# A two-layer transformer kernel: the first expert's weights and rows loaded within attention, and new orders of loads, of GpSimd's steps and of one score sum

## The reference

```
xn = layernorm(x)
x  = x + L0_attn(xn) + L0_ffn(xn)      # low-rank q/kv, rope, causal softmax, 16 heads of 16; 8 experts, top 2, capacity 1280
xn = layernorm(x)
x  = x + L1_attn(xn) + L1_ffn(xn)      # 32 learned patterns, sparsemax over them; 8 experts + shared MLP, masked by top 2

def sparsemax(z):
    z_sorted = -sort(-z); cum = cumsum(z_sorted); k = 1..S
    k_sup = sum(1 + k * z_sorted > cum)
    tau = (cum[k_sup - 1] - 1) / k_sup
    return max(z - tau, 0)
```

## Time and profile before

| | us |
|---|---|
| median of 3 runs | 2135.6 (2132.08 to 2140.5) |
| the profiled execution's own time | 2135.76 |
| its span | 2134.0 |

### The profile page before, as it was taken

The page is one execution under the profiler, slowest core; times in us unless marked ns, Lnnn a source line. Parts: engine busy times, 40 slices in busy tenths (PEclk is TensorE's granted clock), DMA queues, the critical chain, the costliest instruction groups (busy, mean ns, idle before and its releaser), DMA issues. The chain is left out here.

```text
span 2134.0 us, 35062 instructions
## 1 busy us (share of the span) xinstructions
PE 1970.1 (92%) x11874; PEld 1197.7 (56%) x11874; DVE 1537.6 (72%) x3465; ACT 1035.9 (49%) x2246; POOL 517.0 (24%) x932
## 2 busy tenths in 40 slices
PE   7867999999999999999789999996879999999998
PEld 3333333333333333333289999995656777777776
DVE  6858998888888888888045333325669898889983
ACT  3425667777777777777644444443331122221112
POOL 4644223322222222222223333336500000000000
PEclk9968999999999999999989999998889999999998
DMA  5554301111111111110033322215510000000005
GB/s 194 188 155 153 117 16 56 56 42 41 44 43 43 44 43 43 44 43 12 15 110 101 108 85 88 90 45 168 154 45 21 1 20 20 21 20 20 10 11 162
DMA packets 111780, 143.69 MB, mean 67 GB/s; under 512 B 12152, under 2 KB 96768, under 8 KB 111232
## 3 DMA queue, kind: packets, MB, share of 16 engines
q1 hardware_dynamic: 87248, 98.09, 14.2%
q0 software_dynamic: 10400, 31.47, 4.3%
q10 hardware_dynamic: 13968, 12.06, 1.7%
HBM read 85.10 MB, written 56.10 MB: 66 GB/s over the span
## 5 line engine op out<-in xcount | busy, mean ns | idle before, releaser
L830 ACT ACTIVATE at_wt<-at_B 128x512 f32<-128x512 f32 (+3 forms) x1280 | 606.5, 538 | 239.4 <-PE at_B L929 233.4
L1234 DVE TENSOR_REDUCE at_piece_max<-at_A 128x1 f32<-128x512 f32 x768 | 487.3, 683 | 59.4 <-PE at_A L910 57.5
L947 PE MATMUL at_O<-at_wt,at_v 128*32 128x512 f32 (+3 forms) x2560 | 312.3, 540 | 0.0
L735 POOL TENSOR_SCALAR_AFFINE_SELECT at_wt<-at_wt 128x128 f32<-128x128 f32 x512 | 148.0, 294 | 612.9 <-ACT at_wt L830 604.2
L1231 DVE CUSTOM_DVE_ANT_0 at_junk<-at_A,s_hide 128x128 bf16<-128x128 f32 (+3 forms) x512 | 230.2, 487 | 77.4 <-PE at_A L910 77.0
L910 PE MATMUL at_A<-at_k,at_q 96*128 96x512 bf16 (+3 forms) x800 | 275.0, 353 | 8.9 <-DVE at_piece_max L1231 2.6
L929 PE MATMUL at_B<-at_q,at_k 99*128 99x512 bf16 (+3 forms) x800 | 272.7, 348 | 2.0 <-ACT at_wt L830 2.0
L1454 PE MATMUL ex_H<-ex_xT,ex_w_in 128*128 128x256 f32 x1920 | 248.2, 286 | 3.3 <-DVE ex_xT L1561 3.3
L1454 PEld LDWEIGHTS ex_H<-ex_xT,ex_w_in 128*128 128x128 f32 x1920 | 237.4, 193 | 3.6 <-DVE ex_w_out L1566 3.6
L1575 DVE TENSOR_TENSOR ex_h<-ex_act_a,ex_H 128x256 f32<-128x256 f32 x160 | 66.8, 418 | 213.0 <-ACT ex_act_a L1503 212.9
L910 PEld LDWEIGHTS at_A<-at_k,at_q 96*128 96x128 bf16 x800 | 77.6, 97 | 214.4 <-DVE at_piece_max L1234 108.9
(11 more groups left out here) (264 smaller groups left out, 2597.6 us busy)
## 6 DMA issues: line engine op xcount, KB each, us to landing
buf<-at_room POOLq DMA_DIRECT2D x10, 1024.0 KB, 8.9
ex_x<-buf SPq DMA_DIRECT2D x40, 256.0 KB, 2.6
expert_out<-ex_y ACTq DMA_DIRECT2D x40, 256.0 KB, 2.2
ex_raw_in<-in_W_in SPq DMA_DIRECT2D x8, 1024.0 KB, 5.0
q_parts<-parts SPq DMA_DIRECT2D x16, 384.0 KB, 3.4
...
```

The source lines that it names most:

```text
L735: pool.affine_select(block_, block_, [[1, P]], ALU.is_ge, 0.0, base=0, channel_multiplier=-1).then_inc(hidden, 1)
L830: act.activation(wt[(HP * p + h) % NE_][:, q0:CH], pB_of(p, h, u)[:, q0:CH], ACT.Exp, scale=D ** -0.5).then_inc(wt_ready, 1)
L947: pe.matmul(pO[j % 2][rows, q0:CH], vs[n % 3][:, kt // TPC, kt % TPC, :], wt[(HP * p + h) % NE_][:, q0:CH], start=kt < 2 and not late, sto ...
L1234: ins = dve.tensor_reduce(top, pA[slot % NA][:, 0:w], AX.X, ALU.max)
```

## The change

1. Three tiles `raw_in`, `raw_out` and `first_rows` are made ahead of `latents` and live until `experts` ends. In `latents` they are `xn`, two of three `by_cos` and of `by_sin`; in `attention` `q[1]`, `k[1]` and `k[2]`; in `experts` the raw weights and the rows. SP issues expert 0's weight loads and the first two row loads at the end of attention's SP list, once the head pairs that used the tiles are done and all rows are put.
2. First maxima: `pats` gets its own semaphore, so that `pats_turn` waits for it alone; the other nine small loads are waited for from `wq_turn` on. On SP, `mlp_load(3)` to `mlp_load(9)` go ahead of `load(1)`, which is dealt out in four parts between them; `iota` and `below` come after the first max store.
3. GpSimd splits the biases between `low(2)` and `low(6)` and copies the rows before `low(7)`. `low(0)` comes before `diag_q`; the values' product comes after `low(4)`.
4. `layer1`: in the MLP whose DVE list holds the scan, `keep_scores` goes ahead of it.
5. `finish`: Wo shares the semaphore of the first part load.

```diff
-        q = [s["q0"]] + [sb(f"q{i}", [QKS, HP, S], BF16) for i in range(1, 3)]
-        k = [s["k0"]] + [sb(f"k{i}", [QKS, S], BF16) for i in range(1, 3)]
+        q1 = s["raw_in"][:].rearrange("p k n -> p (k n)").bitcast(BF16).rearrange("p (h n) -> p h n", h=HP)
+        k1 = s["raw_out"][:].rearrange("p f e -> p (f e)").bitcast(BF16)
+        k2 = s["first_rows"][:].rearrange("p i t e -> p (i t e)").bitcast(BF16)
+        q = [s["q0"], q1[0:QKS], sb("q2", [QKS, HP, S], BF16)]
+        k = [s["k0"], k1[0:QKS], k2[0:QKS]]
...
             for e in range(NW):
                 mlp_load(e)
-            load(1)
+            for e in range(NW, MLPS):
+                mlp_load(e)
+                if e - NW <= len(RUNS):
+                    load(1, e - NW)
+            max_store(0, 0, M0_SLOT + 2)
             sp.dma_start(iota, d["c_iota"]).then_inc(routing_in, 16)
             sp.dma_start(below, d["c_below"]).then_inc(routing_in, 16)
-            for e in range(NW, MLPS):
-                mlp_load(e)
-            max_store(0, 0, M0_SLOT + 2)
...
+            sp.wait_ge(wt_used, PER_B * (HPAIRS - 2))
+            sp.dma_start(s["raw_in"][:], d["W_in"][0].rearrange("(k p) f -> p k f", p=P)).then_inc(s["w_loaded"], 16)
+            sp.dma_start(s["raw_out"][:], d["W_out"][0].rearrange("(k p) e -> p k e", p=P)).then_inc(s["w_loaded"], 16)
+            sp.wait_ge(wt_used, PER_B * (HPAIRS - 1))
+            for i in range(2):
+                sp.wait_ge(put[i], 16 * 2 * TOPK * (HPAIRS // 2))
+            rows = d["buf"].rearrange("(m t p) e -> m p t e", t=2, p=P)
+            for i in range(2):
+                sp.dma_start(s["first_rows"][:, i], rows[i]).then_inc(s["x_loaded"][i], 16)
...
             def pats_turn():
-                pe.wait_ge(small_in, 16 * 10)
+                pe.wait_ge(pats_in, 16)
...
             def wq_turn():
+                pe.wait_ge(small_in, 16 * 9)
...
-            weights(0)
-            rows(0, 0)
-            rows(1, 1)
             with sp.Fori(0, ROUNDS - 1) as j:
...
+                    scored_next = c + 1 < NCH and SCORE <= i < SCORE + TPC
                     for n, item in enumerate(items_of(i)):
+                        if item == SORTS and scored_next:
+                            keep_scores(c + 1, i - SCORE)
+                            scored_next = False
...
-            pe.wait_ge(wo_in, 16)
+            pe.wait_ge(part_in[0], 32)
```

More of the change, by code:

```diff
@@ L570, in attention @@
         mlp_in = [sem(f"mlp_in{i}") for i in range(NW)]
+        pats_in = sem("pats_in")
         small_in = sem("small_in")
@@ L761, in last_layer @@
                 low(2)
+                pool.wait_ge(bias_in, 32)
+                st.did(pool.tensor_copy(bias_parts[0], both_bias))
                 low(3)
+                st.all_done()
+                st.did(pool.tensor_tensor(bias_rest, both_bias, bias_parts[0], ALU.subtract))
+                low(4)
+                st.all_done()
+                st.did(pool.tensor_copy(bias_parts[1], bias_rest))
                 pool.wait_ge(values_summed, 1)
@@ L780, in last_layer @@
                     st.did(pool.tensor_copy(s["bias_rows"][row], bias_parts[a][row].unsqueeze(2).to_broadcast([1, 2, 2, E])))
+                st.all_done()
+                for e in range(7, MLPS):
+                    low(e)
                 assert st.n == at_pool["bias"]
@@ L860, in mlp_copy @@
                 act.copy(s["down"][:, e], pD.rearrange("p k n -> p (k n)")).then_inc(mlp_kept, 1)
-            act.wait_ge(small_in, 16 * 10)
-            for c in range(EC):
-                st.did(act.copy(bq_wide[:, c], bq[:, c:c + 1].to_broadcast([P, P])))
             act.wait_ge(pe_step, at_pe["pats"])
@@ L867, in _ @@
             mlp_copy(0)
+            act.wait_ge(small_in, 16 * 9)
+            for c in range(EC):
+                st.did(act.copy(bq_wide[:, c], bq[:, c:c + 1].to_broadcast([P, P])))
             act.wait_ge(pe_step, at_pe["wq"])
@@ L1351, in experts @@
         pY = [pb(f"Y{i}", [P, RT, E]) for i in range(2)]
-        w_loaded = sem("w_loaded")
+        w_loaded, x_loaded = s["w_loaded"], s["x_loaded"]
         w_high = sem("w_high")
         w_low = sem("w_low")
-        x_loaded = [sem(f"x_loaded{i}") for i in range(2)]
         xT_made = sem("xT_made")
@@ L2486, in build @@
         keep("bias_rows", [P, 2, 2, E], BF16)
-        with ExitStack() as heads:
-            for name, shape, dt in (
-                ("q0", [STACK + PARTS, HP, S], BF16), ("k0", [STACK + PARTS, S], BF16), ("hide", [P, CH], F32),
-            ):
-                s[name] = heads.enter_context(nc.sbuf_tensor("s_" + name, shape, dt))
-            s["hide_in"] = heads.enter_context(nc.semaphore("hide_in"))
-            s["heads_in"] = [heads.enter_context(nc.semaphore(f"heads_in{i}")) for i in range(3)]
-            latents(nc, d, s)
-            attention(nc, d, s)
-        experts(nc, d, s)
+        with ExitStack() as first:
+            for name, shape in (("raw_in", [P, EC, 2 * F]), ("raw_out", [P, F // P, E]), ("first_rows", [P, 2, 2, E])):
+                s[name] = first.enter_context(nc.sbuf_tensor("s_" + name, shape, F32))
+            s["w_loaded"] = first.enter_context(nc.semaphore("w_loaded"))
+            s["x_loaded"] = [first.enter_context(nc.semaphore(f"x_loaded{i}")) for i in range(2)]
+            with ExitStack() as heads:
+                for name, shape, dt in (
+                    ("q0", [STACK + PARTS, HP, S], BF16), ("k0", [STACK + PARTS, S], BF16), ("hide", [P, CH], F32),
+                ):
+                    s[name] = heads.enter_context(nc.sbuf_tensor("s_" + name, shape, dt))
+                s["hide_in"] = heads.enter_context(nc.semaphore("hide_in"))
+                s["heads_in"] = [heads.enter_context(nc.semaphore(f"heads_in{i}")) for i in range(3)]
+                latents(nc, d, s)
+                attention(nc, d, s)
+            experts(nc, d, s)
         keep("top", [P, TILES, 8])
```

58 lines of the change are left out of this document (28 added, 30 removed).

## The result

| | us |
|---|---|
| the changed kernel, median of 4 runs | 2109.2 (2104.28 to 2111.33) |
| the kernel before, beside it, median of 4 runs | 2133.8 (2131.83 to 2140.5) |
| ratio, 95% interval | 0.9876 (0.9861 to 0.9892) |
| the profiled execution's own time, its span | 2107.26, 2105.6 |

Predicted was 2107.0, within 2099 to 2118: 2109.2 lies in the range and in the forecast's own case (2104 to 2111). The kernel before took 2133.8 us beside it, and not the 2135.6 that the forecast counted from, so the gain is 24.6 us by these medians where 28.6 was forecast.

A forecast was written before the change was run, and what follows sets the result against it. The prediction took PE, busy 92% of the span, as the bound, with time to be had only where it stands still; its terms summed to -28.6 us, from 2135.76 to 2107.2 (2107.0 against the median), range 2099 to 2118.

The forecast's parts named there:

- the forecast's own case: Whole kernel: the terms hold and the time is 2104 to 2111 us, chance 0.66.
- The small loads, -3.0: First maxima: PE no longer stands for the small loads before `pats_turn`, 3.0 us less.
- the fourth MLP's load, -4.0: First maxima: SP issues `mlp(3)`'s weights earlier, so PE's whole 3.97 us stop goes, 4.0 us less.
- GpSimd's order, -6.9: Before round 0: ACT's table load no longer waits for GpSimd's bias rows behind the last `low`, 6.9 us less.
- the clock gives back more: Rival, first maxima: PE's clock rises earlier with the stops gone, 3 to 5 us more gain, 2102 to 2104; chance 0.13.
- Nothing new is late: First maxima: head pair loads between MLP loads delay nothing, each `mlp_load` having over 10 us until needed.
- The clock behind the stop, -1.4: Start of round 0: work lost to the low clock behind the stop comes back, 1.4 us less.
- PE would now stand for well under 2 us, and the level may not fall: Before round 0: PE's stop shrinks from 7.5 us, so the clock may stay up; step behind the 1.4 us gain.
- Attention to the experts, -7.5: Between attention and experts: with expert 0's weights already in SBUF, ACT's first cut starts 7.5 us earlier.
- Layer 1, -6.2: Layer 1: `keep_scores` ahead of the scan spares PE a wait, 1.04 us in each of six chunks, 6.2 us less.
- Finish, +0.4: Last stage: PE's first turn also waits for the first part load, issued 0.43 us after Wo; 0.4 us more.
- two rounds at 1.2 GHz: Rival, attention: the clock stays low for rounds, 36 us each, making the kernel slower, 2150 at two rounds; chance 0.02.

The follow-up runs named there:

- u_sp: Changed kernel with SP's old load order in the first maxima: second head pair's ten loads ahead of the fourth MLP's weights; 2116.4 us, ratio 0.9922.
- b_small: Kernel before plus the separate `pats` semaphore, ACT's bias copies moved, and Wo sharing the first part load's semaphore; 2136.4 us, ratio 1.0000.
- u_experts: Changed kernel with expert 0's weights and the first two row tiles loaded in the experts' block again; 2162.0 us on another chip, ratio 0.9901.
- after: First profile of the changed kernel, with no further edit; the profiled execution took 2107.26 us.
- both_waits: Changed kernel with the head pair's four load parts behind the seventh to tenth MLP loads and PE's Wo wait after two turns; 2114.1 us, ratio 0.9906.
- again: Changed kernel timed and profiled once more, with no edit; 2108.5 us, ratio 0.9865.
- u_scores: Changed kernel with layer 1's copy of the scores behind the scan again; 2163.1 us on another chip, ratio 0.9898.
- fill: Changed kernel with five filler matmuls on PE at the start of round 0; 2155.2 us on another chip, ratio 0.9863.
- spread_fill: Changed kernel with the second head pair's loads spread thinner, PE's Wo wait after two turns, and five filler matmuls in round 0; 2104.0 us, ratio 0.9844.
- u_pool: Changed kernel with GpSimd's old order in the first maxima, bias steps after the last `low`; 2166.0 us on another chip, ratio 0.9902.

## Why the prediction held, and where it didn't

**The small loads, -3.0, and the fourth MLP's load, -4.0.** The sum was about right, its division wrong. The prediction took the stops as independent and subtracted both lengths. But the fourth MLP's weights land at 153.7 us whatever PE does (`u_sp`, `b_small`), because SP issues them behind the second head pair's loads. So the first edit alone gives 0, and the two together, with what little else changed in the stage, 66.6 - 50.9 - 6.0 = 9.7 us, not 7.0; undone one at a time they cost 1.4 and 8.8. The prediction had the row for it (issued at 142.66), and used it only for the second stop.

**GpSimd's order, -6.9.** Measured 6.0; mechanism and place as told.

**The rest of the first maxima.** The 2.7 us over the 7.0 were not traced to a cause. The clock is the obvious one: 0.86 over the stage for 0.68, and the early stretch at 1.2 GHz ends at about 129 us and not at 147. That would be the rival "the clock gives back more". But among profiles of the same order the length doesn't follow the clock: `u_experts` has a mean of 0.79 and took 50.1 us, `after` has 0.86 and took 50.6. DVE is busy 44.80 of 50.10 us there now, so PE's clock can give little more.

**"Nothing new is late": wrong by 1.9 us.** The step gave each `mlp_load` over 10 us until needed, against a longest landing of 10.1. The first number was right: `mlp(5)`'s third load was issued some 12 us before PE wanted it. The second was wrong: it took 13.8 us to land, and 13.5 to 13.7 us at the like place in `both_waits`, `again` and `u_scores`. The row of 10.1 was itself a load with the head pair's loads right behind it, issued at 124.89. What the prediction left out is that the MLPs' loads land later with parts of the pair between them; the third loads of `mlp(4)` to `mlp(6)` took 8.6 to 13.8 us in the changed kernel, and those of `mlp(3)` to `mlp(5)` 4.2 to 6.5 in the kernel before, where nothing stood between them. SP's own time lengthens too: the loads of the head pair took 1.3 to 3.3 us for two DMAs, and one behind them 3.13, where one by itself takes 0.43. Whether the loads ahead or those behind delay a landing was not separated. The wait seems to have cost less than its length: `u_experts`, a single profile, had none and took 50.1 us. The Trainium skill, "Perfetto Trace Analysis", section DMA Instruction — HWDGE, says that such an instruction ends for the profiler when its descriptors have been generated, and that the engines may start on them before, if they don't fit the buffer. The long issue times could stand for a queue that is full, but neither that page nor a run here says so: the runs show the times, not the buffer.

**The clock behind the stop, -1.4: wrong sign.** Attention was 2.5 us longer, 1.24 in round 0 and 1.28 in round 1, by two stretches at 1.2 GHz: 0.75 from 170.6 to 183.0 and 0.88 from 240.2 to 254.2, where before had 0.85 and 1.00. The step that failed is "PE would now stand for well under 2 us, and the level may not fall": it fell in the changed kernel at about 170.0 us, where PE waits 0.2 to 0.8 us at a time and is busy 1.46 of 2.50 us (168.10 to 170.60). That these short waits cause the fall is likely, but not shown: with them filled the level held in `fill` and fell in `spread_fill`, and in `both_waits` it held without fillers. What decides stays open: behind the same 8.1 us stop round 0 took 63.8 us before and 65.1 in `u_pool`, and round 1, with the same instructions, has its slow stretch in six profiles and not in eight. The Trainium skill, "TensorE: Matmul & The Clock Gate", in its section on the second failure mode of the clock gate, describes something near this: in a kernel that cycled through PSUM banks, PE idled briefly between groups of matmuls, often enough that the level went up and down. The trace fits it, with no PE wait over 0.8 us at the fall. By the rule that the prediction cited, that long waits do it, 1.4 us would have come back.

**Attention to the experts, -7.5.** Measured 7.5 in the profile and 7.4 by undoing it. The first cut is 5.2 us behind attention's last instruction, as told, and the loads lengthen neither of the last two rounds.

**Layer 1, -6.2.** Measured 5.8 and, in `again`, 6.3; undone 5.8. The 0.05 given back at the next MLP are 0.18 us, a second short wait in most chunks where one was forecast. Chunk 0 is unchanged (5.33 us for 5.32), as told.

**Finish, +0.4.** Measured +0.7; the wait behind Wo's issue grew from 2.77 to 3.55 us, within the bound of 1.

**The whole.** Terms off by -2.1 (first maxima), +3.9 (attention), -1.8 (latents) and some tenths cancel between the two profiled executions, which are 28.5 us apart; the medians are 24.6 apart. So the larger terms, the stops, came out by their mechanisms, and that the sum did too, with the clock's term of the wrong sign, is luck. One sum among the rivals is wrong: two rounds at 1.2 GHz would give 2107 + 2 x 36 = 2179 us, not 2150. No round ran so.

The best version is `spread_fill`: 2104.0 us, ratio 0.9844 (0.9828 to 0.9861), beside 2108.5 and 0.9865 (0.9849 to 0.9882) for the changed kernel on the same chip. It is the lowest of all medians there, but the intervals overlap.
